# Feed-forward with experts: when the next batch's rows are normalised, turned and split

## The reference

```python
def _layernorm(x, axis=-1, eps=1e-05):
    m = jnp.mean(x, axis=axis, keepdims=True)
    v = jnp.var(x, axis=axis, keepdims=True)
    return (x - m) / jnp.sqrt(v + eps)

def _L0_ffn_ref(x, Wr, Wg, Wu, Wd):      # E = 8 experts, K = 2, F = 256, D = 256
    probs = jax.nn.softmax(x @ Wr, axis=-1)
    topk_w, topk_idx = jax.lax.top_k(probs, K)
    topk_w = topk_w / jnp.sum(topk_w, axis=-1, keepdims=True)
    output = jnp.zeros_like(x)
    for i in range(E):
        sel = topk_idx == i
        w_i = jnp.sum(topk_w * sel.astype(x.dtype), axis=-1, keepdims=True)
        h = jax.nn.silu(x @ Wg[i]) * (x @ Wu[i])
        output = output + w_i * (h @ Wd[i])
    return output

x = x + _L0_ffn_ref(_layernorm(x), L0_ffn_Wr, L0_ffn_Wg, L0_ffn_Wu, L0_ffn_Wd)
```

## Time and profile before

| | us |
|---|---|
| median of 3 runs | 3156.69 (3152.51 to 3158.48) |
| profiled execution, its own time | 3153.1 |
| its span, first to last instruction | 3150.4 |
| TensorE busy | 2854.7 (91%) |
| VectorE busy | 1659.8 (53%) |
| GpSimd busy | 992.2 (31%) |
| ScalarE busy | 842.7 (27%) |
| granted TensorE clock, mean | 0.926 |

### The profile page before, as it was taken

The page is one execution under the profiler, slowest core; times in us unless marked ns, Lnnn a source line. Parts: engine busy times, 40 slices in busy tenths (PEclk is TensorE's granted clock), DMA queues, the critical chain, the costliest instruction groups (busy, mean ns, idle before and its releaser), DMA issues. The chain is left out here.

```text
span 3150.4 us, 45793 instructions
## 1 busy us (share of the span) xinstructions
PE 2854.7 (91%) x15592; PEld 1944.5 (62%) x15592; DVE 1659.8 (53%) x4517; ACT 842.7 (27%) x1368; POOL 992.2 (31%) x1105
## 2 busy tenths in 40 slices
PE   7999999998999999999979999999999758888876
PEld 3444458886656555788867777777777634443444
DVE  5566646666555646466644333333333565555555
ACT  2343344442101101344422222222222002222310
POOL 0000036765444445567631122222221011121211
PEclk8999999999999999999989999999999657888975
DMA  3000020000000000100000000000000000000000
GB/s 138 1 0 0 0 100 1 0 0 0 1 0 0 0 0 0 81 0 0 0 14 14 1 14 15 14 1 14 15 1 1 24 0 1 1 0 1 1 0 27
DMA packets 6288, 37.96 MB, mean 12 GB/s; under 512 B 272, under 2 KB 4368, under 8 KB 4496
## 3 DMA queue, kind: packets, MB, share of 16 engines
q1 hardware_dynamic: 6160, 36.34, 3.0%
HBM read 34.24 MB, written 2.10 MB: 12 GB/s over the span
## 5 line engine op out<-in xcount | busy, mean ns | idle before, releaser
L590 PE MATMUL banks<-back 32*128 32x512 f32 (+3 forms) x1088 | 364.6, 598 | 31.4 <-DVE back L600 22.1
L365 PE MATMUL banks<-moe_parts 128*128 128x512 f32 x1536 | 368.4, 396 | 15.3 <-POOL moe_parts L445 8.5
L817 ACT ACTIVATE back<-banks 128x1024 f32<-128x1024 f32 (+3 forms) x256 | 217.0, 863 | 459.7 <-PE banks L711 459.5
L365 PEld LDWEIGHTS banks<-moe_parts 128*128 128x128 f32 x1536 | 287.7, 191 | 78.5 <-issue 20.8
L1433 PE MATMUL banks<-lin_parts 128*128 128x512 f32 x1152 | 307.5, 413 | 18.9 <-DVE lin_parts L1684 15.5
L1619 DVE TENSOR_TENSOR ffn_pack<-banks,back 128x512 f32<-128x512 f32 x128 | 88.5, 691 | 351.5 <-PE banks L1446 351.4
L711 PE MATMUL banks<-back 32*128 32x512 f32 (+3 forms) x1024 | 242.3, 586 | 19.8 <-DVE back L833 12.5
L1433 PEld LDWEIGHTS banks<-lin_parts 128*128 128x128 f32 x1152 | 213.6, 194 | 67.4 <-issue 21.0
L590 PEld LDWEIGHTS banks<-back 32*128 32x128 f32 x1088 | 135.2, 199 | 187.9 <-DVE back L604 77.8
L1749 POOL TENSOR_TENSOR ffn_pack<-ffn_pack 128x256 f32<-128x256 f32 x112 | 82.9, 740 | 498.9 <-ACT ffn_pack L1582 498.9
L604 DVE TENSOR_REDUCE back<-banks 128x1 f32<-128x512 f32 x272 | 176.5, 687 | 79.9 <-PE banks L590 75.4
(11 more groups left out here) (235 smaller groups left out, 5307.0 us busy)
## 6 DMA issues: line engine op xcount, KB each, us to landing
back<-p_raw SPq DMA_DIRECT2D x8, 1024.0 KB, 4.8
back<-p SPq DMA_DIRECT2D x1, 7696.0 KB, 21.5
ffn_pack<-ffn SPq DMA_DIRECT2D x1, 6144.0 KB, 26.8
back<-p SPq DMA_DIRECT2D x1, 5152.0 KB, 15.2
back<-p SPq DMA_DIRECT2D x2, 1792.0 KB, 8.2
out<-x SPq DMA_DIRECT2D x1, 2048.0 KB, 7.5
x<-x_in SPq DMA_DIRECT2D x1, 1536.0 KB, 12.7
small_pack<-small SPq DMA_DIRECT2D x1, 619.0 KB, 4.9
```

Source lines behind the costliest of these rows:

```text
L365: mm = nc.tensor.matmul(bank[:], up[:, n % 2, a, which, kd, :], xp[:, b, kd, :], start=((a, b, kd) == (0, 0, 0)), stop=((a, b, kd) == (1, ...
L590: nc.tensor.matmul(bank[:, 0:n], qs[head_rows[j], hg, qi * P:(qi + 1) * P], ks[head_rows[j], hg, 0:n], start=True, stop=True).then_inc(D.f ...
L817: nc.scalar.activation(pt[:, (kt % 2) * 2 + pair, :, q0:T], two[:, :, q0:T], ACT.Exp, scale=0.25).then_inc(A.free.s, 2)
```

## The change

- TensorE: `turn_xn` moves from e = 7 to e = 6, where it stands behind the two units of expert 7 and ahead of the down product of expert 6.
- VectorE: two steps of the normalisation stand at each of e = 0, 1 and 2 and the last step at e = 3; `keep_xt` moves to e = 6, ahead of `weigh(6)`.
- ScalarE and GpSimd: the split of the rows moves from the beginning of a batch to the end of the batch before, behind the last hidden part; ScalarE waits there until the second turned bank is free. For a layer's first batch it stands ahead of the loop. The last batch of a layer splits rows too, which nothing reads.

```diff
@@ TensorE
                         for f in range(FC):
                             if e + 1 < E2:
                                 unit(e + 1, f)
-                        if e + 1 == E2:
+                        if e + 2 == E2:
                             turn_xn(nc, c, pe, it)
                         down(e)
@@ ScalarE
-                with act.Fori(0, B) as it:
-                    act.wait_ge(D.free.s, D.all_free(it))
+
+                def x_hi():
                     for kd in range(KD):
                         nc.scalar.activation(xp[:, 0, kd, :], c.xt[:, kd, :], ACT.Identity).then_inc(c.x_hi.s, 1)
+
+                act.wait_ge(D.free.s, D.all_free(0))
+                x_hi()
+                with act.Fori(0, B) as it:
                     act.wait_ge(c.lg_ready.s, c.lg_ready.at(it, 1))
...
                     hidden_hi(UNITS - 1)
+                    act.wait_ge(D.free.s, D.released(it, "xt", KD - 1))
+                    x_hi()
@@ GpSimd
-                with pool.Fori(0, B) as it:
+
+                def x_lo(it, first):
                     for kd in range(KD):
-                        pool.wait_ge(c.x_hi.s, c.x_hi.at(it, kd + 1))
+                        pool.wait_ge(c.x_hi.s, c.x_hi.at(it, first + kd + 1))
                         nc.gpsimd.tensor_tensor(xp[:, 1, kd], c.xt[:, kd], xp[:, 0, kd], ALU.subtract)\
                             .then_inc(c.x_lo.s, 1)
 
+                x_lo(0, 0)
+                with pool.Fori(0, B) as it:
...
                     hidden_lo(UNITS - 1)
+                    x_lo(it, KD)
@@ VectorE
                     for e in range(E2):
                         if e + 1 < E2:
                             hidden(e + 1)
-                            norm[e]()
-                        else:
+                            for step in norm[2 * e:2 * e + 2]:
+                                step()
+                        if e + 2 == E2:
                             keep_xt(nc, c, dve, it)
                         weigh(e)
@@ end of the layer
         c.up_hi.base += 2
         c.up_lo.base += 2
+        c.x_hi.base += KD
+        c.x_lo.base += KD
```

## The result

The changed kernel takes 3131.91 us (median of 4 runs, 3128.02 to 3133.71) beside 3156.43 for the kernel before: ratio 0.9922, interval 0.9905 to 0.9939, faster by 24.5 us where 9.9 were forecast and 3139 was the lower end of the range. Its profiled execution took 3133.7, with a span of 3131.4, 19.0 less than before.

A forecast was written before the change was run, and what follows sets the result against it. TensorE was taken to lose time where batches meet, waiting 2.03 for the normalised rows; eight joints at 1.05 (8.4) and 1.5 of clock make 9.9, giving 3146.8 us by the median, range 3139 to 3154.

The forecast's parts named there:

- What the change takes away: At eight batch ends, TensorE's 2.03 wait for the normalised rows goes; GpSimd then holds down product 7; gain 1.05 each.
- R: Moment the next batch's router product starts on TensorE; forecast to come 7.9 after the last up product's end, instead of 8.95.
- U: Moment a batch's last up product ends on TensorE, from which the forecast counts each joint between batches.
- The split of the rows: Between batches, TensorE's 0.36 wait for the split goes but gains 0, since a chain behind the router product sets the start.
- The doubled steps: Two normalisation steps per expert on VectorE cost 0, since the added root step fits into a pause of GpSimd.
- The rival on the slower side: In steps 1 and 2, doubled normalisation steps wait for GpSimd and hold PSUM banks; 11.7 slower, 3168; chance 0.07.
- The clock at the joints: Down product 7 took 4.61 at two joints under a fallen clock; gain 1.5 taken, bounds 3.0 gain to 8.9 loss.
- The sum: Whole kernel: 8 x 1.05 = 8.4, with 1.5 of clock 9.9 gained; 3146.8 by the median.
- The clock: TensorE's granted clock falls behind idle stretches at joints; fewer falls gain 1.5, bounds 3.0 gain to 8.9 loss.
- That all the waiting goes: Rival: at the joints all idle time and the clock's 3.0 go, 21.4 in all, giving 3135.3; chance 0.07.
- That the joint doesn't shorten: Rival: later GpSimd hidden parts or new clock falls swallow the gain at the joints; 3151 to 3157; chance 0.24.

The follow-up runs named there:

- gate first: The changed kernel with VectorE's first multiplication of a batch moved ahead of the last steps of its choice of experts; 3133.4 us.
- normalisation only: The kernel before with only two normalisation steps per expert, so rows are written in step 3, not 6; turn and split unmoved; 3136.3 us.
- both: The changed kernel with GpSimd's last hidden parts ahead of the next batch's weights and VectorE's first multiplication ahead of the choice's last steps; 3128.8 us.
- all but normalisation: The changed kernel with one normalisation step per expert as before, so the earlier turn waits for rows written in step 6; 3189.4 us.

## Why the prediction was wrong

**Right, by its own steps.** *What the change takes away*: 1.0 to 1.1 for each joint was forecast, 1.0 measured; the wait ahead of down product 7 at 0.59 (forecast 0.5 to 0.8), R at U + 7.96 (7.8 to 8.0), the bank's wait at 0.43. *The split of the rows*, costed at nothing: R to the fourth up product 12.18 before and after, and gate first shows the chain that sets it. *The doubled steps*, costed at nothing. VectorE, GpSimd and TensorE in the second batch, step 1, changed kernel:

```profile
544.59 0.33 DVE L161 TENSOR_SCALAR var_eps<-mv 128x4 f32<-128x4 f32 x1
...
544.96 1.22 DVE L162 TENSOR_SCALAR var_half<-var_eps 128x4 f32<-128x4 f32 x1
...
546.09 1.31 POOL L471 TENSOR_TENSOR moe_parts<-ffn_pack,moe_parts 128x512 fp32r<-128x512 f32 x1
546.28 1.15 DVE L164 TENSOR_SCALAR rstd<-rstd 128x4 int32<-128x4 int32 x1
...
547.47 0.16 DVE L170 TENSOR_TENSOR rstd_sq<-rstd 128x4 f32<-128x4 f32 x1
547.66 0.16 DVE L171 TENSOR_TENSOR rstd_sq<-rstd_sq,var_half 128x4 f32<-128x4 f32 x1
547.86 0.16 DVE L172 SCALAR_TENSOR_TENSOR rstd<-rstd_sq,rstd 128x4 f32<-128x4 f32 x1
548.24 1.66 DVE L530 SCALAR_TENSOR_TENSOR x<-banks,moe,x 128x256 f32 x4 [0.22 <-DVE rstd L172]
...
549.72 1.30 POOL L466 TENSOR_TENSOR moe_parts<-ffn_pack,moe_parts 128x512 fp32r<-128x512 f32 x1 [2.32 <-ACT moe_parts L430]
549.89 0.69 DVE L520 TENSOR_TENSOR moe<-moe,banks 128x512 f32<-128x512 f32 x1
...
552.51 3.13 PE L379 MATMUL banks<-moe_parts 128*128 128x256 f32 x24
...
561.13 1.09 PE L379 MATMUL banks<-moe_parts 128*128 128x256 f32 x7
```

The guess waits out GpSimd's instructions as before, until 546.09 + 1.31 = 547.40; the three links of the root step then take 0.16 each in GpSimd's pause, the weighing starts at 548.24, and the next down product comes at 552.51 after 543.88: 8.63, the old period. Step 2, with its two root steps, keeps it too (561.13, 8.62 later). The multiplication at 549.89 begins right behind the weighing, 6.01 after the down product's start, where it was 6.00 before: it isn't even the 0.3 late that was forecast. The rival on the slower side needed six or seven waits of 1.22; there are two in this step (1.22 and 1.15). *The clock at the joints*: no down product 7 took 4.61 any more, so both falls went; 1.5 was taken, 3.0 was the bound. *The sum* for the expert layers: 9.9 forecast, 10.2 measured; that they lie so near is partly luck, since 1.0 for each of eight joints and 3.0 of clock are 11.0, and the batches themselves became some 0.8 longer, most of it in each layer's first.

**Wrong.** The step that failed is *The clock*, and through it *The sum*. I weighed falls of the clock at the joints alone, "a gain of 3.0 (both go), a loss of 8.9", and took every layer behind as unchanged. The term that was left out is the untouched layers' own clock: 11 us less at the changed kernel's timing, by the medians. The profile's page of the kernel before had shown where to look, in its row of the granted clock by 40 slices, in tenths:

```profile
PEclk8999999999999999999989999999999657888975
```

In the last nine slices it lies between 0.5 and 0.9, where the slices that lie wholly in an expert layer (the seventh to ninth, the 18th to 20th) show 0.9 or more. Of the 14.9 between the forecast of 3146.8 and the measured 3131.9, this term is 11.4. Another 3.2 are the point that the sum started from, a median of three runs (3156.69) where 21 gave 3153.5, and 0.3 are the expert layers.

**The other rivals.** That all the waiting goes gave 3135.3, near the measured time and for the wrong reason: the joint's wait did not go, it moved to GpSimd, and the 0.36 went to the split of weights. That the joint doesn't shorten is refuted: R came 1.0 earlier at every joint that had no fall before, and down product 7 takes 3.12 to 3.14 at all eight.

**Open.** Why a given timing brings many or few falls is not settled. A start earlier by 10 us doesn't do it by itself: normalisation only has the same expert layers and a rest of 2525; gate first and both start their later layers earlier still and have 2530 and 2533. And with the pauses ahead of latent attention the two kernels answered differently. These kernels also ran on different chips, so a share of the chip isn't ruled out.

## What to carry to other kernels

Ask what waits behind the wait that goes: here GpSimd's last instruction took over at 1.0 of 2.03, and one reordering of its queue gave another 0.85. Before a gain is credited to a change, compare the layers that it doesn't touch; where their length moves, count only the touched ones, repeat the change with a pause behind it, and look whether the kernel before reaches the same low time in some of its executions. A part that looks like the change's aim (the turn, the split) may add nothing, or cost, without the small move beside it.

## What was not expected of the hardware

With a pause of 1.1 us at the end of the second layer, one execution of the changed kernel, its slowest, had the fifth and the seventh layer, 900 and 1800 us later, 13 us longer than the profile without the pause (870.99 to 876.62 and 477.84 to 485.46), with the same instructions and the granted clock 0.82 to 0.81 in the second; by the medians the pause cost 6 beyond its own length. The unchanged kernel before took 3138 in some executions and 3158 in others, with the granted clock at 0.932 and 0.923. And a wait of 5.12 on TensorE cost another 1.2 to 2.6 behind it, at a granted clock of 0.68 to 0.82, in the joints of all but normalisation.
